# A three-layer transformer kernel on eight cores: small steps into attention, transposes by transfers, BF16 copies in DRAM

## The reference

```python
x = x + 0.5 * ffn(layernorm(x))
x = x + attn(layernorm(x))
x = x + 0.5 * ffn(layernorm(x))

def ffn(x):            # D = 2048, K = 8 experts of rank R = 64
    h = relu(x @ W1 + b1)
    alpha = softmax(h @ W2 + b2)               # over the 8 experts
    vx = einsum('krd,bsd->bskr', V, x)
    return einsum('bsk,bskd->bsd', alpha, einsum('kdr,bskr->bskd', U, vx))

def attn(x):           # 16 heads of 128
    q, k, v = heads(x @ Wq), heads(x @ Wk), heads(x @ Wv)
    # 64-token blocks; a block sees the blocks at most 2 away
    return (softmax(q @ k.T / sqrt(128) + mask) @ v) @ Wo
```

## Time and profile before

| | before |
|---|---|
| runs | 1811.45, 1816.94, 1996.73 us |
| profiled execution | 1813.04 us |
| span of its slowest core (core 3) | 1811.4 us |
| spans of all cores | 1794.1 to 1811.4 us |
| mean granted TensorE clock, core 3 | 0.989 |
| TensorE busy | 1736.0 us, 96% |
| VectorE, ScalarE, GpSimd busy | 43%, 24%, 11% |
| DMA | 218.37 MB, mean 121 GB/s |

### The profile page before, as it was taken

One profiled execution on the slowest core, in us unless ns is written; L12 is line 12 of the kernel. 1 busy time (PEld: TensorE's weight loads), 2 busy tenths in 40 slices (PEclk: granted clock), 3 DMA queues, 4 the chain that ended last, 5 costly groups with the idle time before them and its releaser, 6 DMA issues.

```text
span 1811.4 us, 34807 instructions; the slowest of 8 cores (1794.1 to 1811.4 us)
## 1 busy us (share of the span) xinstructions
PE 1736.0 (96%) x12724; PEld 1149.9 (63%) x12724; DVE 787.0 (43%) x1633; ACT 429.8 (24%) x1035; POOL 192.2 (11%) x318
## 2 busy tenths in 40 slices
PE   3999999989899999999999999979999999999998
PEld 3867655545577777777777777755444455576556
DVE  5047657506354555545454545434213334143421
ACT  2312311111233333333333333321000011111111
POOL 2001022000111111111111111110000000011000
PEclk9999999989999999999999999989999999999999
DMA  9946566499954545555555456999890684154211
GB/s 208 180 103 215 159 140 176 119 58 164 187 83 75 80 72 84 74 75 78 72 81 77 68 82 95 127 146 226 219 328 25 114 154 143 44 155 126 94 70 48
DMA packets 256217, 218.37 MB, mean 121 GB/s; under 512 B 194480, under 2 KB 232368, under 8 KB 244784
## 3 DMA queue, kind: packets, MB, share of 16 engines
q1 hardware_dynamic: 215056, 120.62, 31.1%
q0 software_dynamic: 38976, 89.70, 28.2%
q10 hardware_dynamic: 2016, 5.81, 1.0%
HBM read 168.93 MB, written 59.24 MB: 126 GB/s over the span
## 4 chain that ended last, share of the span: by engine, by line
PE 84%; SPq 7%; DMA 4%; DVE 3%; issue 1%; ACT 1%; POOL 0%; DVEq 0%; ACTq 0%; POOLq 0%
PE R L721 23%; PE R L385 17%; PE R L711 12%; PE R L977 12%; SPq L102 6%; PE R L437 5%; PE R L469 4%; PE pX L385 4%; PE R L850 2%; DVE lnb L305 2%; DMA W1a<-w 2%; DMA PTs<-Pn 1%; PE pX L437 1%; PE pX L469 1%; PE pX L810 1%; PE pS L810 1%
## 5 line engine op out<-in xcount | busy, mean ns | idle before, releaser
L711 PE MATMUL R<-wvS,xn2T 128*128 128x256 bf16 x2176 | 255.4, 275 | 3.3 <-DVE Qb L733 3.3
L721 PE MATMUL R<-xn2T,wkS 128*128 128x384 bf16 (+1 forms) x1536 | 251.5, 317 | 0.0
L721 PE MATMUL R<-xn2T,wqS 128*128 128x384 bf16 (+1 forms) x1536 | 240.5, 310 | 0.0
L711 PEld LDWEIGHTS R<-wvS,xn2T 128*128 128x128 bf16 x2176 | 214.1, 99 | 35.7 <-issue 3.9
L385 PE MATMUL R<-xnTa,W1a 128*128 128x256 bf16 (+2 forms) x1648 | 205.3, 283 | 24.2 <-issue 9.0
L977 PE MATMUL R<-Wo,Ob 128*128 128x512 bf16 x1024 | 222.6, 379 | 0.0
L721 PEld LDWEIGHTS R<-xn2T,wkS 128*128 128x128 bf16 x1536 | 150.1, 98 | 82.1 <-issue 0.6
L721 PEld LDWEIGHTS R<-xn2T,wqS 128*128 128x128 bf16 x1536 | 151.0, 99 | 75.5 <-issue 3.1
L385 PEld LDWEIGHTS R<-xnTa,W1a 128*128 128x128 bf16 x1648 | 141.6, 99 | 69.3 <-issue 25.8
L385 PE MATMUL R<-xnTc,W1c 128*128 128x384 bf16 (+1 forms) x1232 | 185.1, 307 | 0.0
L977 PEld LDWEIGHTS R<-Wo,Ob 128*128 128x128 bf16 x1024 | 99.9, 98 | 118.9
(11 more groups left out here) (100 smaller groups left out, 1684.0 us busy)
## 6 DMA issues: line engine op xcount, KB each, us to landing
x1d<-Xa SPq DMA_DIRECT2D x16, 1024.0 KB, 4.2
y<-Xc SPq DMA_DIRECT2D x16, 1024.0 KB, 4.5
Xa<-x POOLq DMA_DIRECT2D x10, 1024.0 KB, 9.2
Xc<-x1d POOLq DMA_DIRECT2D x9, 1024.0 KB, 19.6
xn2d<-xna SPq DMA_DIRECT2D x17, 512.0 KB, 5.3
W1a<-w POOLq DMA_DIRECT2D x16, 512.0 KB, 43.4
Wo<-wo POOLq DMA_DIRECT2D x32, 256.0 KB, 5.7
x2d<-Xc SPq DMA_DIRECT2D x8, 1024.0 KB, 15.2
```

What stands on the lines that cost most here:

```text
L711: tok = p.mm(lambda e, c=c, o=o: e.matmul(bank[:, 0:256], xn2T[:, o:o + 128], wvS[s][:, c * 256:(c + 1) * 256], start=(c == 0), stop=(c == ...
L721: tok = p.mm(lambda e, c=c: e.matmul(bank[:, 0:w], wS[:, c * 256 + k * 128: c * 256 + (k + 1) * 128], view(xn2T, a * D + c * 128, (D, n), ...
```

## The change

It has these parts.

1. `zturn` turns z by a DMA transpose on the SP queue and no longer by TensorE and ScalarE. There are three `zt` and four `zT` buffers. In `vu`, all turns are issued as the z come, `up(k - 3)` runs ahead of the turn of z(k), and between the last V group and the remaining U groups stands a filler: the first W1 group of the next block, or, in the last block of the first layer, the K projections of group 0 (`first_k`). The last group of the final layer has no filler.
2. The logits run one W1 group later (`logits(1)`).
3. `xn2T` is filled in small steps: tiles 0 to 8 one at a time after W1 groups 2 to 10 of the last block; 9 and 10 after its U groups; tiles 11 to 16 are turned straight out of SBUF (`turn_xn2`) and are not stored to `xn2d`. The first K, Q and V slabs come in eight parts each, K during the block before, Q and V during the last block. x1 of tiles 14 and 15 is stored from GpSimd's queue. The Q of pair 0, group 0 is scaled on ScalarE.
4. V and U are copied in BF16 from SBUF to DRAM in block 1 (eight DMAs), W1 in blocks 2 and 3 (sixteen), all issued by ScalarE. GpSimd copies Wo from DRAM to DRAM with the cast, up to five parts in group 0 of pairs 0 to 6. The later loads of Wo, W1, V and U read these copies.
5. The norms of tiles 8, 9 and 10 are turned by DMA.

```diff
@@ zturn
-            bank, done = transposes(lambda j: z[:, j * 128:(j + 1) * 128], 4, [tok])
-            self.zt.give(z, done)
             zT, free = self.zT.take()
-            end = p.op("scalar", lambda e: e.copy(
-                zT[:, :], pT[:, bank * 1024: bank * 1024 + 512]), done, *free)
-            tbank["ended"][bank] = end
+            end = p.dma_turn(S(zT.name), view(zT, 0, (128, 4), (1, 128)), z[:, :], tok, *free)
+            self.zt.give(z, end)
@@ vu
-                if k >= 1:
-                    turn(k - 1)
-                if k >= 2:
-                    up(k - 2)
-            if n == 2:
-                up(0)
-            turn(n - 1)
-            for k in range(max(1, n - 2), n):
+                if k >= 3:
+                    up(k - 3)
+                zT[k] = self.zturn(*z)
+            if filler:
+                filler()
+            for k in range(max(0, n - 3), n):
                 up(k)
@@ copies
+    def copy_w1(e):
+        copy_tok["w1"] = p.dma("scalar", S("w1b"), rows(w1b, e), W1a[e][:, :], W1atok[e])
@@ seam
+    def turn_xn2(t, *tokens):
...
+        b, tok = ln2_b[t]
+        end = p.dma_turn(S(f"tx{place[t]}"), view(xn2T, t * D, (128, 16), (1, 128)), b[:, :],
+                         tok, copy_tok["w1"], copy_tok["vu"], *tokens)
...
         if last_blk:
-            for e, gs in ((4, (0,)), (8, (1, 2)), (12, (3,))):
-                for q in gs:
-                    pairs.append((e, lambda q=q, e=e: load_xn2T(q, first.w1_done[(blk, e - 1)])))
+            pairs += [(3 + i, lambda i=i: slab_part("q", 11, i, e=3 + i)) for i in range(8)]
+            pairs += [(8 + i, lambda i=i: slab_part("v", 12, i, e=8 + i)) for i in range(8)]
+            pairs += [(t + 2, lambda t=t: load_xn2T(t, first.w1_done[(blk, t)]))
+                      for t in range(9)]
         run_items(blk, [(0, e) for e in range(16)], at_hooks(pairs))
+        vu_a(blk, {})
         if last_blk:
-            load_xn2T(4, first.w1_done[(blk, 15)])
-        vu_a(blk, {})
+            for t in (9, 10):
+                load_xn2T(t, first.w1_done[(blk, 15)])
+            for t in (11, 12, 13):
+                turn_xn2(t, first.w1_done[(blk, 15)])
@@ Wo
+    def cast_wo(cg, part, *tokens):
...
+        copy_tok["wo"] = p.dma("gpsimd", S("wob"), rows(wob, cg)[:, a:a + 1024],
+                               rows(dwo, cg)[:, a:a + 1024], *tokens)
```

More of the change, by code:

```diff
@@ L206, in build_nc @@
     hTa = [at(f"hTa{s}", 200704 + 768 * s, 384, BF16) for s in range(3)]
-    zta = [at(f"zta{s}", 203008 + 1024 * s, 512, BF16) for s in range(2)]
-    zTa = [at(f"zTa{s}", 205056 + 1024 * s, 512, BF16) for s in range(3)]
+    zta = [at(f"zta{s}", 203008 + 1024 * s, 512, BF16) for s in range(3)]
+    zTa = [at(f"zTa{s}", 206080 + 1024 * s, 512, BF16) for s in range(4)]
     xn2T = at("xn2T", 0, NT * D, BF16)
@@ L234, in build_nc @@
     hTc = [at(f"hTc{s}", 205824 + 768 * s, 384, BF16) for s in range(3)]
-    ztc = [at(f"ztc{s}", 208128 + 1024 * s, 512, BF16) for s in range(2)]
-    zTc = [at(f"zTc{s}", 163840 + 1024 * s, 512, BF16) for s in range(3)]
+    ztc = [at(f"ztc{s}", 163840 + 1024 * s, 512, BF16) for s in range(3)]
+    zTc = [at(f"zTc{s}", 166912 + 1024 * s, 512, BF16) for s in range(4)]
     small = [210400]
@@ L394, in w1, with logits, logits_of @@
             self.banks.ended[i] = relu
-            self.late = (blk, i0, n, e, h, relu)
-        def logits(self):
-            if self.late is None:
-                return
-            blk, i0, n, e, h, relu = self.late
-            self.late = None
+            self.late.append((blk, i0, n, e, h, relu))
+        def logits(self, keep):
+            while len(self.late) > keep:
+                self.logits_of(*self.late.popleft())
+        def logits_of(self, blk, i0, n, e, h, relu):
             col = (blk % 2) * 40 + i0 * 8
@@ L478, in u, with vu @@
             return add
-        def vu(self, blk, places, xs, added, hooks):
+        def vu(self, blk, places, xs, added, hooks, filler=None):
             n = len(places)
-            zs, zT = {}, {}
+            zT = {}
             def hook(key):
@@ L617, in w1a, with call @@
         first.w1(blk, t - BLOCKS[blk][0][0], n, place[t], e, [xnT_tok[q] for q in range(t, t + n)])
+    def call(f, *args):
+        return lambda: f(*args)
     def vu_a(blk, hooks):
         ts = tiles_a(blk)
-        first.vu(blk, [place[t] for t in ts], [xa(t) for t in ts], added_a(blk), hooks)
+        filler = call(w1a, blk + 1, 0, 0) if blk + 1 < len(BLOCKS) else first_k
+        first.vu(blk, [place[t] for t in ts], [xa(t) for t in ts], added_a(blk), hooks, filler)
     def at_hooks(pairs):
@@ L670, in build_nc @@
         (23, call(ln2_store, 4)), (26, call(ln1_act, 9)), (27, call(ln1_half, 10)),
-        (29, call(ln1_turn, 9)), (31, call(ln1_act, 10))])
+        (29, call(ln1_turn, 9)), (31, call(ln1_act, 10))]
+        + [(3 + 4 * i - i // 7, call(copy_vu, i)) for i in range(8)])
     run_items(1, items, hooks)
@@ L688, in build_nc, with load_xn2T @@
     xn2T_tok = {}
-    def load_xn2T(g, *tokens):
-        for t in range(GROUPS[g][0], sum(GROUPS[g])):
-            xn2T_tok[g] = p.dma_turn(S(f"lxn{g}"), view(xn2T, t * D, (128, 16), (1, 128)),
-                                     rows(xn2d, t), xn2_tok[t], *tokens)
+    def load_xn2T(t, *tokens):
+        xn2T_tok[GROUP_OF[t]] = [p.dma_turn(
+            S(f"lxn{GROUP_OF[t]}"), view(xn2T, t * D, (128, 16), (1, 128)), rows(xn2d, t),
+            xn2_tok[t], copy_tok["w1"], copy_tok["vu"], *tokens)]
+    def turn_xn2(t, *tokens):
+        if t not in ln2_b:
+            flush_ln()
+        b, tok = ln2_b[t]
+        end = p.dma_turn(S(f"tx{place[t]}"), view(xn2T, t * D, (128, 16), (1, 128)), b[:, :],
+                         tok, copy_tok["w1"], copy_tok["vu"], *tokens)
+        xn2T_tok.setdefault(GROUP_OF[t], []).append(end)
+        norm.xn.give(b, end)
     kq_end = {}
@@ L704, in proj @@
         w = n * 128
-        i, bank, ended = banks3.next()
-        p.wait("tensor", slab_tok[(kind, pr)], xn2T_tok[g], ended)
+        i, bank, ended = banks.next()
+        p.wait("tensor", slab_tok[(kind, pr)], *xn2T_tok[g], ended)
         if kind == "v":
@@ L746, in free_then, with slab_part @@
         def free_then(t):
[L747 to L752 removed]
+            ln2(t, call(load_x, t + 7, "gpsimd") if t + 7 < NT else None)
+        def slab_part(name, t, part, blk=blk, e=0):
+            load_slab(name, 0, part, *x_last[t], first.w1_done[(blk, e - 1)])
         pairs = []
@@ L786, in build_nc @@
     pt_read = [None] * 4
+    p.wait("vector", copy_tok["vu"])
+    p.wait("scalar", copy_tok["vu"])
     for b in range(3):
@@ L894, in build_nc @@
     wo_tok = [None] * 4
+    wo_casts = deque((cg, part) for cg in range(4) for part in range(8))
+    def cast_wo(cg, part, *tokens):
+        a = part * 1024
+        copy_tok["wo"] = p.dma("gpsimd", S("wob"), rows(wob, cg)[:, a:a + 1024],
+                               rows(dwo, cg)[:, a:a + 1024], *tokens)
     def load_wo(cg, part, *tokens):
@@ L1092, in done_c, with w1c @@
         return run
+    def w1c(i, e):
+        ts = list(qtiles(ORDER[i]))
+        final.w1(i, 0, len(ts), place_c[ts[0]], e, [xnTc_tok[t] for t in ts])
     for i, g in enumerate(ORDER):
```

97 lines of the change are left out of this document (55 added, 42 removed).

## The result

The changed kernel takes 1794.7 us (median of 7 runs, 1790.97 to 1812.9); the kernel before, timed beside it, 1811.45. The ratio is 0.9935, 95% interval 0.9908 to 0.9962: 0.65% faster, less than the 2% that count as a difference. The time is 21 us above the forecast of 1774 and outside its own range of 1762 to 1786, though inside the 1752 to 1802 given for 8 times in 10. The prediction had given 0.64 to a gain of more than 2%.

A forecast was written before the change was run, and what follows sets the result against it. TensorE was taken as the bound, busy 1736.0 of 1811.4 us, with gains from its work and its waits. The terms summed to -39.5 us, span 1771.9, forecast 1774 us; own range 1762 to 1786, 1752 to 1802 for 8 times in 10.

The forecast's parts named there:

- The step that failed: Copies of V, U and W1 on ScalarE's queue: bounds 0 and about 7 us, taken as 1 us lost.
- the filler: Before the U groups: 2.6 us of cover for z's transfer, hidden with 3 us to spare with three tiles.
- two signs of being wrong: TensorE waiting for z in the middle blocks, or for Relu behind a copy that ScalarE issues; no size given.
- The seam: From the first layer's last block into attention: costs 26.4 us, 11.7 remaining after the change, gain 14.7.
- The stall on VectorE: Start of pair 0: the `Qb` wait moves by one group, 4.5 us plus 2.8 on the slower clock.
- Rival A: The seam keeps its price, `PTs` behind Wo's casts, stores and turns on SP: 1789 or 1794 us; chance 0.22.
- Wo in BF16: End of attention: `PTs` waits of 10.4 us and about 2 of slow matmuls, 2.5 kept as residue; gain 10.
- z and the norms off TensorE: z: 7.3 us saved, 1.6 of waits gone, 2 lost at the last group; norms 8 to 10: 2.7 plus 3.2.
- The logits: One W1 group later: three of the 4.5 us that TensorE waits for Relu should go.
- B: z starves behind norm turns on SP at 18.2 us each; TensorE stands for 52 us: 1826 us; chance 0.07.
- C: No new waits: VectorE and z in time, end of attention free, residues of 11.7 and 2.5 go: 1757 us; chance 0.14.
- D: Each transpose removed gives back five times its 0.055 us, through latency on the path: 1734 us; chance 0.02.

The follow-up runs named there:

- Experiment 1: Changed kernel without the BF16 copies of W1, V and U, the last layer loading the FP32 inputs; 1889.6 us, no interval.
- 6: Changed kernel without BF16 copies of W1, V and U, and with norms of tiles 8 to 10 turned by TensorE; 1814.3 us, ratio 0.9963.
- experiment 2: Changed kernel with no filler in blocks 0 to 3 of the first layer, `first_k` kept; 1789.9 us, ratio 0.9896.
- experiment 9: Changed kernel; W1, V, U cast DRAM to DRAM by GpSimd during attention, Wo casts in pairs 1 to 6, `Pn` zeros on GpSimd, tile 10 turned earlier; 1781.1 us.
- kernel 5: Changed kernel with z turned by TensorE and ScalarE again, each turn one V group late; 1793.5 us, ratio 0.9910.
- experiment 4: Changed kernel without the casts of Wo, pair 7 loading the FP32 input; 1794.5 us, ratio 0.9912.
- experiment 7: Changed kernel with Wo's casts in pairs 1 to 6 and none in pair 0; 1790.1 us, ratio 0.9889.
- kernel 11: As experiment 9, but all 80 casts spread over groups 1 to 5 of pairs 1 to 6, none in group 0; 1775.3 us, ratio 0.9807.
- 10: As experiment 9, but without the filler at the first four block boundaries; 1779.1 us, ratio 0.9825.

## Why the prediction was wrong, point by point

**The step that failed** is the one on the copies: "In the blocks they share the DMA engines with loads of x and the norm's turns. Nothing on TensorE needs them", priced at 1 us for ScalarE's issuing. It looked for the cost at the issuing engine, where there is none: no TensorE wait for a Relu grew. It did not ask who waits for the norm's turns. With that goes the filler: the prediction counted it as 2.6 us of cover for z, and never as work whose own operand is now wanted some 10 us earlier on a queue that the same change slows. In the first layer 1.3 us were to be won beside the stop on core 3 told below. With the copies the mean was 4.4 to 10.2 us longer than before (418.5 to 424.3 against 414.1); without them, in kernels 1 and 6, it is 2.0 and 0.3 us shorter (some 1.5 us of the 414.1 are that stop on one core of eight), so the rest of the sum for this stage holds within about 2 us. Experiment 1 gives 6.4 to 12.2 us for the copies, experiment 2 gives 2.9 to 8.7 for the filler beside them (the two overlap and do not add up), and in experiment 9 both are gone once the copies are moved. The prediction had named two signs of being wrong, a wait for z in the middle blocks and one for Relu behind a copy. Neither came; the wait that did, for `xnTa`, was not on its list.

**The core.** The sum was made on the slowest core of one execution and held on the core of that number (-39.4 forecast, -37.0 measured), which is luck: its first layer gave 5.2 us less and its attention 2.7 more than forecast, and in other runs of the changed kernel core 3 took up to 1788.9 us. Second, 11.8 us of the sum were a stop of 9.04 us in a W1 group with its slow matmuls that no other core had in that execution (core 1 had one of 1.9). On the others there was less to win, and the time is that of the slowest. In the runs of the kernel before that the ratios count, each core from 1 to 7 is the slowest at some time and core 3 lies between 1774.5 and 1812.2 us. The cause of the stop is open: the trace names none, and kernel 5 has one of 5.8 us on core 2. A wait that one core in eight has is worth at most the distance to the next slowest.

**The seam.** Right in its parts. The nine turns take 5.3 us each (under 6 forecast). z is in time, where 4.4 us of loss were kept. The stall on VectorE moved by one group as said, with 6.2 us and 1.8 of slow matmuls for 4.5 and 2.8; it stands behind the K cast on ScalarE and not behind the scaling of Q, and is just over the 3 to 6 us given. Rival A's condition came true in part: `PTs` behind Wo's casts, 6.0 to 10.8 us on three of eight cores; experiments 4 and 7, without these casts, have no such wait on any core. They are not its only cause: kernel 11, without them too, has one of 5.5 us on core 0. Rival A's time (1789 to 1794) is what came out, but mostly for another reason, the first layer.

**Wo in BF16.** Right in kind: the waits at the end of attention are gone, and some come back with FP32 (experiment 4), but half of what the kernel before had. Together with its casts in pair 0 the part won nothing in attention, where 10 us were forecast; with the casts moved (experiment 7) it wins 3.6 us against FP32 (785.2 against 788.8). The output stage gains 2.8 us more from it (226.8 against 224.0), which the sum had not.

**z and the norms off TensorE.** Busy time fell as forecast, but the time did not follow for z: experiment 5, with z back on TensorE, is not slower, where the sum had 7.3 + 1.6 - 2 = 6.9 us for it. Norms 8 to 10: 7.1 for 5.9, on the condition, not seen, that the loads of the last layer are small (experiment 1). The last group's first U waits 2.92 us (2 to 3 forecast). The logits: 3.2 us for 3 on core 0, in part by luck. The kernels whose first layer has no long `xnTa` wait (1, 9 and 10) show 3.5 us of Relu waits on most cores, for 3.4 to 4.9 before, so the later logits alone give about 1 us there.

**Rivals B, C and D.** z did not starve, and the nine turns are far from B's 9.5 us each. Against B the prediction argued that small parts hold up a turn less than one slab does. In the block before the last it is not so: the second three turns beside the K slab in eight parts and without copies (kernels 1 and 9) take 14.3 to 18.7 us, beside the one slab before 10.2 to 13.5. C's "no new waits" is what kernel 11 comes near to, at 1775 and not 1757. D is answered in experiment 5.

## What to carry to other kernels

Work put ahead of a wait as cover has operands of its own: find what makes them, and when, before it is counted. A background transfer that nobody waits for is costed by what it slows, in this kernel the DMA transposes; put it where none is on the path. Make the sum for the second and third slowest core as well, and count a stop that only one core shows no higher than the gap to the next. Before a stage is compared, look how far the same stage of the same program differs between two executions: here 5.8 us in the mean of the first layer, about half of the largest effect looked for.
